# A recurrent kernel on one core: moving the scaling of its outputs from GpSimd to VectorE, and the second half of their evaluation to a later place

## The reference, cut to what matters

```python
q = silu(conv(x @ Wq)); k = silu(conv(x @ Wk)) * DK ** (-0.5); v = silu(conv(x @ Wv))
alpha = sigmoid(x @ Wa + ba); beta = sigmoid(x @ Wb + bb)
def step(S, inps):
    qt, kt, vt, at, bt = inps
    err = einsum('bhvk,bhk->bhv', S, kt) - vt
    S = at * S - bt * (err[..., None] * kt[:, :, None, :])
    return S, einsum('bhvk,bhk->bhv', S, qt)
mu = mean(o, -1); var = mean(square(o - mu), -1)
o = (o - mu) * rsqrt(var + 1e-05) * ln_w + ln_b
g = sigmoid(x @ Wg)
o = (o * g).reshape(B, T, H * DV)
return o @ Wo
```

## Time and profile before

| | |
|---|---|
| median of 3 runs | 3104.82 us (3100.4 to 3105.01) |
| profiled execution, its own time | 3104.56 us |
| its span | 3102.8 us |
| recurrent part | about 400 to 1804 us of the span |
| one unit there | about 42.6 us |
| PE busy from 600 to 1700 us | 98 to 99% |
| POOL in `scaled`, line 1766 | 217.5 us, 256 instructions |

### The profile page before, as it was taken

How to read it: one execution, slowest core, us unless ns; L and a number is a source line. 1 busy time by engine, 2 the same in 40 slices (tenths; PEclk the granted TensorE clock), 3 DMA queues, 4 the chain that set the end, 5 groups by cost and what they waited for, 6 DMA issues and landing times. The chain is left out here.

```text
span 3102.8 us, 61493 instructions
## 1 busy us (share of the span) xinstructions
PE 3032.5 (98%) x23896; PEld 2510.4 (81%) x23896; DVE 1973.9 (64%) x3434; ACT 1651.2 (53%) x4011; POOL 1503.9 (48%) x2479
## 2 busy tenths in 40 slices
PE   8999989999999999999999899999999999999999
PEld 7888867888888888888888678788888888888887
DVE  6111267777777777777777433746666666666666
ACT  5221358777778877778777633443333333222222
POOL 2222337777777777777777544323333223222212
PEclk9999999999999999999999999999999999999999
DMA  2101111111111111111111154311011111000004
GB/s 93 31 21 28 63 62 42 46 56 52 54 44 49 49 56 56 54 49 44 54 56 46 49 189 149 103 31 31 28 31 44 35 31 31 21 22 27 26 16 163
DMA packets 130243, 165.69 MB, mean 53 GB/s; under 512 B 9936, under 2 KB 72144, under 8 KB 129920
## 3 DMA queue, kind: packets, MB, share of 16 engines
q1 hardware_dynamic: 120592, 144.49, 15.4%
q10 hardware_dynamic: 9296, 17.04, 1.5%
q0 software_dynamic: 64, 0.23, 0.0%
HBM read 127.91 MB, written 33.82 MB: 52 GB/s over the span
## 5 line engine op out<-in xcount | busy, mean ns | idle before, releaser
L1488 DVE SCALAR_TENSOR_TENSOR b_zt<-b_rx,b_cw,b_zt 128x512 f32<-128x512 f32 x576 | 476.3, 827 | 21.7 <-POOL b_rx L1685 3.2
L70 PE MATMUL bank<-b_XH,b_wh 128*128 128x512 f32 x1024 | 456.9, 446 | 8.7 <-ACT b_zt L1238 7.0
L72 PE MATMUL bank<-b_XH,b_wl 128*128 128x512 f32 x1024 | 404.0, 394 | 0.0
L71 PE MATMUL bank<-b_XL,b_wh 128*128 128x512 f32 x1024 | 403.0, 394 | 0.0
L70 PE MATMUL bank<-b_XH,b_qh 128*128 128x512 f32 x1024 | 399.2, 390 | 1.4 <-DVE b_g L2641 1.4
L71 PE MATMUL bank<-b_XL,b_qh 128*128 128x512 f32 x1024 | 398.6, 389 | 0.0
L72 PE MATMUL bank<-b_XH,b_ql 128*128 128x512 f32 x1024 | 398.6, 389 | 0.0
L2751 POOL TENSOR_TENSOR b_QHL<-b_qhd,b_QHH 128x512 fp32r<-128x512 f32 x124 | 176.6, 1428 | 453.3 <-ACT b_QHH L2519 450.9
L2519 ACT CAST b_QHH<-b_qhd 128x512 fp32r<-128x512 f32 x124 | 76.9, 622 | 293.9 <-PE bank L72 176.9
L72 PEld LDWEIGHTS bank<-b_XH,b_wl 128*128 128x128 f32 x1024 | 193.1, 189 | 44.4
L1731 POOL TENSOR_TENSOR b_PR<-b_A,b_T 128x15 f32<-128x15 f32 (+7 forms) x480 | 173.8, 362 | 110.7 <-issue 75.9
(11 more groups left out here) (269 smaller groups left out, 7682.5 us busy)
## 6 DMA issues: line engine op xcount, KB each, us to landing
b_abc<-tmp_a SPq DMA_DIRECT2D x64, 256.0 KB, 3.4
b_gbc<-tmp_g SPq DMA_DIRECT2D x64, 256.0 KB, 3.8
tmp_og<-b_gg SPq DMA_DIRECT2D x64, 256.0 KB, 2.4
b_mo<-tmp_og SPq DMA_DIRECT2D x64, 256.0 KB, 3.2
b_wr<-in_Wk SPq DMA_DIRECT2D x16, 256.0 KB, 3.1
b_wr<-in_Wq SPq DMA_DIRECT2D x16, 256.0 KB, 4.1
b_wr<-in_Wv SPq DMA_DIRECT2D x16, 256.0 KB, 2.7
b_wr<-in_Wg SPq DMA_DIRECT2D x16, 256.0 KB, 4.1
```

The costliest lines, as they stand in the source:

```text
L70: e.do.matmul(out, wh, xh, start=first and k == 0, stop=False)
L71: e.do.matmul(out, wh, xl, start=False, stop=False)
L72: m = e.do.matmul(out, wl, xh, start=False, stop=last and k == n - 1)
L1488: e.do.scalar_tensor_tensor(out=z[:, :], in0=rx[:, j:j + 512], scalar=cw[:, u // 2, KIND[name[0]], j:j + 1], in1=z[:, :], op0=ALU.mult, op ...
```

## The change

Three things are moved; nothing is added to the arithmetic and nothing taken away. The four-piece function `scaled` goes from POOL's round to DVE's, its first call between `masked(i, 3)` and `masked(i, 4)`, its second behind `masked(i, 7)`. PE's `turn(i - 3, 1)` and ACT's `turned(i - 3, 1)` go behind the second step of the chain, `chain2(i - 2, 1)`. DVE's `gated(., 1)` goes from the end of a round to behind `chain1(i - 2, 2)` of the next.

```diff
@@ attn0_pe, one round
         project(i, "k0", 1, 2)
-        turn(i - 3, 1)
         project(gate_unit(i), "g0", 3, 4)
         project(i, "k0", 2, 3)
         chain1(i - 2, 1)
         project(i, "k0", 3, 4)
         turn_kv(i - 1, 0)
         chain2(i - 2, 1)
+        turn(i - 3, 1)
         turn_kv(i - 1, 1)
         project(gate_unit(i), "g1", 0, 1)
@@ attn0_act, one round
         turned_kv(i - 2, 3)
-        turned(i - 3, 1)
         chain4(i - 2, 0)
         gate(gate_unit(i), 0)
         chain2(i - 2, 1)
+        turned(i - 3, 1)
         cut_next("g", i - 1)
         taken(i, "k0")
@@ attn0_dve
+    def scaled(u, b):
+        if not live(u):
+            return
+        e.wait_ge("nw", 12 * u + 12)
+        e.wait_ge("mu", u + 1)
+        for ch in range(4):
+            i = 4 * b + ch
+            r = e.do.tensor_scalar(t["OS"][:, b, ch, :], t["OS"][:, b, ch, :], ss[:, 4, i:i + 1], ss[:, 2, i:i + 1], ALU.subtract, ALU.mult)
+        r.then_inc(S["osc"], 1)
...
-    for i in range(NU + 2):
+    for i in range(NU + 3):
         chain3(i - 2, 1)
         decay(i, 0)
         chain1(i - 2, 2)
         ahead(i - 2, 0, 1)
+        gated(i - 3, 1)
...
         masked(i, 3)
+        scaled(i - 2, 0)
         masked(i, 4)
         decay(i, 6)
         decay(i, 7)
         masked(i, 5)
         masked(i, 6)
         masked(i, 7)
+        scaled(i - 2, 1)
         gated(i - 2, 0)
...
         taps(i, "v1")
-        gated(i - 2, 1)
@@ attn0_pool, one round (the function scaled is taken out there)
         tail(i - 1, "q1")
-        scaled(i - 3, 0)
         ones(i - 1)
         cut_next("v", i - 1)
-        scaled(i - 3, 1)
         decayed_q(i - 1, 0)
```

More of the change, by code:

```diff
@@ L1757, in root @@
         e.do.tensor_tensor(y, y, a, ALU.mult).then_inc(S["nw"], 1)
[L1759 to L1767, removed]
     def ahead(u, c0, c1):
```

## The result

The changed kernel takes 3150.7 us (median of 4 runs, 3149.0 to 3151.3) against 3104.2 us of the kernel before (4 runs, 3100.4 to 3105.0): a ratio of 1.0154, 95% interval 1.0141 to 1.0166. It is 46.5 us slower; the forecast was +61.6. The span of its profiled execution is 3149.5 us, 46.7 more than before.

A forecast was written before the change was run, and what follows sets the result against it. PE, busy 98% of the span, was taken as the bound, so only its waits count. 31.8 + 7.8 + 10.5 + 18 - 6 - 3.5 + 3 = +61.6 us, 3166 us; 8-in-10 range 3130 to 3182, own range 3150 to 3180.

The forecast's parts named there:

- part 2: Scaled pieces on DVE delay scans, masks and `R`; PE's second chain step loses 0.7 us quiet, 1.2 with casts: +10.5, +18.
- part 3: PE's 8.9 us of waits at the turn for POOL's scaled outputs mostly go: -6 us, bounds 0 and -8.9.
- part 1: ACT's output copy waits for the later turn, so its gate holds `g1`: +31.8 us; `v0` with casts: +7.8.
- the gate product: DVE's `gated(., 1)`, moved and not added, with its later store on SP: costed at nothing.
- second wait: In units with casts, PE waits at `v0` for ACT's late `z3`: 0.5 us in 15 units, +7.8 us.
- S: Start of the chain's second step on PE; the forecast had ACT's gate end at S + 2.13, `g1` start at S + 2.27.
- the signs: Expected in the changed profile: among others ACT's copy waiting 2 to 3 us for the turn, units of about 44.6 us.
- Part 4: End of the kernel: pieces faster on DVE than POOL, -3.5 us; delays showing in full at the last unit, +3 us.
- A: Rival: pieces fit DVE's idle time and meetings miss, only ACT's hold costs: +33, 3138 us; chance 0.25.
- B: Rival: ACT's hold is hidden because `gt` is needed later, only the pieces cost: 3127 us; chance 0.03.
- C: Rival: faster, scaled pieces ready earlier, turns wait no more and nothing new waits: 3091 us; chance 0.04.
- D: Rival: delays of part 2 pile up on part 1, or a piece costs 0.30: 3182 us and over; chance 0.08.

The follow-up runs named there:

- the kernel with a place of its own: Changed kernel with a separate 1 KB per partition for the first output chunk of every second unit: 3114.8 us against 3101.8 before the change, ratio 1.0044.
- the doses: Changed kernel with the second turn 0.43 us earlier or later on PE: 3128.6 us (1.0081) and 3160.7 us (1.0188), both against 3102.9 before the change.

## Why the prediction was right, and where it was off

The direction, the main cause and the range (3130 to 3182) held. The time itself was 15 us too high, at the lower edge of the forecast's own 3150 to 3180, and that it came so near was in part luck: part 2 was 22 us too high, part 3 took away 4 us too little, and against that part 1 was 3 us too low, the gate product's 5 us were missing, and 3 us of the difference lie outside the units, where I had put nothing.

**Part 1, the hold: right.** 1.06 us a unit forecast, 1.09 and 1.22 measured; second wait 0.5, measured 0.53; together 39.6 against 42.7 us. The steps stand in the rows one by one: turn end to copy, two copies, gate, `g1`. In the quiet unit the gate ends at S + 2.26 and not at S + 2.13, because the turn ends at S + 1.05 and ACT starts 0.09 behind it. That the single buffer is the link is shown by the kernel with a place of its own (-34 us) and by the doses. The 0.14 us taken from ACT's end to PE's start was 0.05 at the gate (1124.02 to 1124.07), which makes up for most of that, and 0.15 at `v0`. Two of the signs were sized wrong: ACT's copy waits 4.18 us for the turn and not 2 to 3, and a unit takes 44.0 us and not 44.6 (42.5 before, by the same mark).

**Part 2, the pieces on DVE: the term that failed.** Forecast +28.5 us, measured +6.6. The price of a piece was right (four in 1.05; 1.03 to 1.10), and so was the meeting in quiet units (1.7 us; 1.77). What failed was the step from there to PE: "PE loses 0.7 us in a quiet unit, 15 x 0.7" and "by the same steps I take 1.2 us" with casts; it was 0.25 and 0.19. In quiet units the median `chain3` starts 2.88 us ahead of the time at which PE would be at its second step, where by my steps it would be 2.65; `R` ends 0.17 us behind that time and not 0.54; and PE starts 0.06 us behind `R`, where I had taken 0.14. So little was missing that 0.7 us shrank to 0.25. And not all units meet: of 25 `decayed_q` that overlap the scans 14 lengthened them, 10 of 13 in quiet units and 4 of 12 in units with casts. In units with casts I had both the piece and the scans slowed. The piece met the cut (four in 1.76 us), but `decayed_q` came only 0.55 us after the start of the scans, too late to hold them:

```profile
1070.41 0.72 DVE L1499 TENSOR_TENSOR_SCAN b_D<-b_abc,b_cst 128x128 f32<-128x128 f32 x2
```

```profile
1070.96 1.28 POOL L1714 TENSOR_TENSOR b_QG<-b_KQA,b_gbc 128x512 f32<-128x512 f32 x1 [1.84 <-issue]
```

The DMA of `gbc` is issued behind `decay(i, 3)`, so it moves with DVE: that scan took 1.29 us beside a cut, the issue stood at 1067.01, and 3.8 us later is 1070.8. I had taken its time from a quiet unit. And what is left of the term is as much the turn's slot that went from ahead of the chain's step as the pieces: the later turn alone loses 0.28 us there with casts, the pieces alone nothing in either.

**Part 3, the waits that go:** -6 forecast, -9.9 measured, -7.5 with the new wait of 0.16 us at the first turn. I argued that the listed gap holds also a weight load, so less is lost than is listed; it is the other way round.

**Part 4, the end:** -3.5 and +3; measured -3.1 and +2.7.

**The gate product, costed at nothing:** +4.8 us in the changed kernel, 6.6 by itself. I looked at who waits for the store on SP, and not at who waits for its landing: ACT, which reuses `gg1`.

**The rivals.** A, the hold alone at 3138, was nearer to the truth in its mechanism than part 2, and in its number 13 us off against 15; of its two assumptions the pieces' small cost held, and "the meetings miss" did not. B and C are refuted: the pieces alone do not cost, and the hold is not hidden. For D nothing speaks; the delays overlap and do not pile up.

## What to carry to other kernels

When an operation is moved behind another, look for the buffer that it frees: whoever refills that buffer waits now, and so does everything behind it in that engine's order, whether it has to do with the buffer or not. Follow this down to each thing that the bounding engine needs from there, and check the later ones with the first wait taken away; else a repair only moves the wait. And a transfer that only stores a result is not free to come late if its source is written again.

## What the runs showed of the hardware

**Who starts first has the port.** In the changed kernel scans and `decayed_q` overlap 25 times between 500 and 1700 us. Where `decayed_q` begins before the scan pair, or at most 0.18 us after it, the pair takes 1.67 to 1.78 us instead of 0.73 (14 times). With starts from 0.05 us before to 0.14 us after, nine of these times, POOL takes longer as well, 1.36 to 1.53 us instead of 1.28. That fits a `decayed_q` that waits for the first scan and then holds the second one, but no row shows it inside an instruction. Where it begins 0.24 us or more after the pair, the scans keep their 0.72 or 0.73 us (11 times), and at distances of 0.24 to 0.26 us it is POOL that takes longer, 1.54 to 1.57 us. The masks, which read PSUM, take 1.61 us for six in both cases, and `R` 0.61. Single scans that begin while POOL cuts weights take 0.86 us in the median and up to 1.29 instead of 0.42, and four pieces 1.76 instead of 1.10, though a piece has one tensor in SBUF as its input. SBUF — State Buffer of the Trainium skill, section "SBUF: two separate sides", calls the ports that VectorE and GpSimd share an exclusive lock that goes to the one that starts first; scans, masks and `decayed_q` agree with it. That the pieces are held too agrees only if their scalars, which lie in SBUF too, count as a second input, or if they run in a two-port mode; no run here tells these apart.

**Listed idle time of PE is too short.** Where 0.82, 0.94 and 0.32 us are listed, the starts say 1.07 to 1.09, 1.22 and 0.53. Short waits are not listed at all. In this quiet unit the last transpose ends 0.10 us before the chain's second step, where such a step else starts 0.11 us after the transpose's start; 0.26 us were lost:

```profile
1034.19 0.27 PE L980 MATMUL bank<-b_cst,b_vt 128*128 128x128 f32 x1
1034.56 0.71 PE L1090 MATMUL bank<-b_R,b_MF 128*128 128x128 f32 x4
```
